# Expert weights split inside the expert loop, and a conditioning stage computed in transposed form

## What is computed

```
t   = lora(x) + emb                      # per batch, rank 16
q   = ffn0(t)                            # int8-style fake quantisation, 256 -> 704 -> 256, SiLU gate
x1  = x + q                              # 4096 rows of 256
h   = relu(x1 @ W1 + b1)                 # per batch, 64 wide
y   = x1 + h @ W2 + b2
z   = (y - mean(y)) * rsqrt(var(y) + 1e-5) * gamma + beta
logits = z @ Wr                          # 9 experts, the best two, softmax over them
moe = sum_k w_k * (silu(z @ Wg_k) * (z @ Wu_k)) @ Wd_k
out = x1 + moe
```

## Time and profile before

| | us |
|---|---|
| median of 3 runs (lowest, highest) | 803.58 (802.08, 804.01) |
| the profiled execution, its own time | 805.9 |
| its span | 804.1 |
| TensorE busy in the span | 672.1 (84%) |
| VectorE busy | 647.7 (81%) |
| ScalarE busy | 449.8 (56%) |
| GpSimd busy | 288.6 (36%) |

### The profile page before, as it was taken

One profiled execution on the slowest core, in us unless ns is written; L12 is line 12 of the kernel. 1 busy time (PEld: TensorE's weight loads), 2 busy tenths in 40 slices (PEclk: granted clock), 3 DMA queues, 4 the chain that ended last, 5 costly groups with the idle time before them and its releaser, 6 DMA issues.

```text
span 804.1 us, 16215 instructions
## 1 busy us (share of the span) xinstructions
PE 672.1 (84%) x4260; PEld 428.0 (53%) x4264; DVE 647.7 (81%) x1881; ACT 449.8 (56%) x801; POOL 288.6 (36%) x262
## 2 busy tenths in 40 slices
PE   6784876588877876219999999999999999999993
PEld 1212332354554545206767767776777767677762
DVE  6687888688999987837888888888888888888862
ACT  2675887578666645115555556555565655556540
POOL 1000455054688887720223222222322223232222
PEclk9665898578678665559999999999999999999996
DMA  6795112244566646863668677566666776766662
GB/s 211 267 363 192 62 37 75 66 151 144 173 192 186 184 141 189 260 223 65 104 103 114 105 99 121 101 114 106 112 108 96 114 104 111 114 104 107 109 89 38
DMA packets 163207, 107.63 MB, mean 134 GB/s; under 512 B 112940, under 2 KB 153012, under 8 KB 163124
## 3 DMA queue, kind: packets, MB, share of 16 engines
q1 hardware_dynamic: 149108, 88.10, 46.3%
q0 software_dynamic: 13440, 17.97, 12.8%
q10 hardware_dynamic: 576, 0.53, 0.2%
HBM read 50.31 MB, written 30.30 MB: 100 GB/s over the span
## 4 chain that ended last, share of the span: by engine, by line
PE 40%; issue 8%; DMA 6%; DVE 1%; POOLq 1%; ACT 1%; SPq 1%; POOL 0%; DVEq 0%; ACTq 0%
PE ps L1036 25%; PE ps L1078 13%; DMA out<-small 4%; PE ps L1020 2%; DMA rows<-small 1%; POOLq L1103 1%; POOL out L1096 0%; DVE small L1047 0%; SPq L972 0%; ACT small L1052 0%; DMA small<-rows 0%; ACT small L1060 0%; POOLq L73 0%; SPq L973 0%; DVE small L1066 0%
## 5 line engine op out<-in xcount | busy, mean ns | idle before, releaser
L1036 PE MATMUL ps<-big,small 128*128 x1728 | 273.2, 315 | 1.6 <-ACT small L1042 1.0
L1096 POOL DMA_INDIRECT out<-small x72 | 111.9, 1554 | 337.2 <-DVE small L1092 295.5
L1036 PEld LDWEIGHTS ps<-big,small 128*128 128x128 f16 x1728 | 164.0, 98 | 93.1 <-issue 2.6
L1078 PE MATMUL ps<-big,small 128*128 (+1 forms) x1224 | 156.4, 277 | 4.7 <-DVE small L1092 4.7
L1052 ACT ACTIVATE small<-small 128x704 f16<-128x704 f32 x72 | 56.9, 790 | 169.0 <-DVE small L1047 169.0
L1078 PEld LDWEIGHTS ps<-big,small 128*128 128x128 f16 (+1 forms) x1224 | 117.7, 99 | 34.3 <-issue 21.2
L1066 DVE SCALAR_TENSOR_TENSOR small<-small 128x64 f16<-128x64 f32 (+1 forms) x144 | 77.8, 582 | 18.8 <-ACT small L1060 18.8
L1047 DVE SCALAR_TENSOR_TENSOR small<-ps,small 128x704 f32<-128x704 f32 x72 | 68.5, 951 | 18.8 <-PE ps L1036 18.8
L858 POOL DMA_INDIRECT rows<-small x64 | 73.5, 1148 | 19.9 <-issue 16.7
L1060 ACT ACTIVATE small<-small 128x704 f16<-128x704 f32 x72 | 63.5, 882 | 16.2 <-DVE small L322 16.2
L609 PE MATMUL ps<-small 128*128 128x512 bf16 x188 | 50.2, 428 | 15.5 <-DVE small L585 9.0
(11 more groups left out here) (156 smaller groups left out, 1038.5 us busy)
## 6 DMA issues: line engine op xcount, KB each, us to landing
small<-rows SPq DMA_DIRECT2D x72, 130.0 KB, 2.1
big<-in_Wg SPq DMA_DIRECT2D x9, 704.0 KB, 4.2
big<-in_Wu SPq DMA_DIRECT2D x9, 704.0 KB, 4.2
big<-in_Wd SPq DMA_DIRECT2D x9, 640.0 KB, 8.2
halves<-big SPq DMA_DIRECT2D x6, 704.0 KB, 4.0
small<-in_xT SPq DMA_DIRECT2D x8, 512.0 KB, 4.0
small<-in_x SPq DMA_DIRECT2D x16, 256.0 KB, 4.1
out<-big SPq DMA_DIRECT2D x16, 256.0 KB, 4.2
```

The costliest lines, as they stand in the source:

```text
L1036: m = put("pe", ("gate", "up")[j], [tk["xsT", t], free, *wload, hl["hi", 26], hl["lo", 26]], lambda e, h=h, k=k, xp=xp, wp=wp, n=n: e.matm ...
L1078: tk["dn", t] = put("pe", "dn", [tk["hT", t], mk("yw", t - 1)], lambda e, n=n, w=w, hc_=hc_, wp=wp, c=c: e.matmul(ps[:, 7, 0:H], hTE[t % 3 ...
L1096: tk["add", t] = dma("pool", f"add{t % 2}", [tk["yw", t], *out_ready], lambda e: e.indirect_dma_start(out=out[:, :], out_offset=bass.Indir ...
```

## The change

- The nine early pieces are no longer split in the front, nor are any in the conditioning stage. `half_load` reads an expert's weights by its number from a table `permI`, sorted by how many rows the first six batches send to an expert. Six pieces are loaded after step 16; three are split before tile 0, the other 24 within the iterations 0 to 46 (`begin`), one about every two iterations: sum of squares in iteration `begin`, column sum (now bf16, one product), scale and high half in the next one, the low half in two parts in the two after that. The stores to HBM and the nine reloads of parts are gone.
- Tiles 0 to 4 belong to the fullest expert and start after step 19, before the last batch is routed; the tables are computed in iterations 0 to 3. Tile 5 waits for all scatters and paddings.
- The down product of the first network gives the transposed block; `st_x1T` adds x transposed. `st_px` is a real product with the identity, which carries nine logit columns and one column for the mean (`TG`), and the adapter product adds to the same PSUM banks (`W2S` with the same ten columns). So the transposes of the normalised rows, their evacuation and the logit products go. Their coefficients are made once by 16 small products (`through_adapter`) behind the gate and up stage, four elementwise products and `centre` in the front.
- The variance is a sum of squares on ScalarE (`st_squares`, one step after the adapter product); gamma is applied on VectorE with the evacuation, the scale and beta in one more operation each (`st_aff`); GpSimd has the power and the scatters left. The clip after quantisation is half on ScalarE (a second 128 x 1536 operation, from block 2 on) and half on VectorE.
- All rows share one power of two, worked out at the head of the conditioning stage from gamma and beta, so that the row scales of a tile (L999 to L1006) go. The row weights (L1084 to L1088) move to GpSimd (`side`, `weigh`).

The core of the diff:

```diff
-        hl, stored = {}, {}
+        hl = {}
+        AHEAD = 6
...
-            return bigf[:, o:o + PW[pieces[n][1]]]
+
+            k, j = divmod(n, 3)
+            o = 3 * EW + n * SLOT if n < AHEAD else 8 * EW + sum(PW[:j])
+            return raw8[:, 0:PW[j]] if k == E - 1 else bigf[:, o:o + PW[j]]
...
         def halves_out(n):
 
-            e_, j = pieces[n]
+            k, j = divmod(n, 3)
             w = PW[j] // 2
-            if n < EARLY:
-                o = (EARLY + n % 4) * SLOT
-                hi, lo = bigf[:, o:o + w], bigf[:, o + w:o + 2 * w]
...
+        def half_sum(n, waits=()):
+
+            m = put("act", "hsum", [hl["in", n], *waits], lambda e: e.activation(
+                halves_out(n)[0], slot_in(n), ACT.Square, accum_out=col(wsum, n)))
+            hl["sum", n] = put("act", "hsum", [m], lambda e: e.activation(col(wsb, n), col(wsum, n), ACT.Copy))
+
+        def top(n):
+            return ps[:, 7 if n < 3 else 5, 0:1]
+
+        def half_top(n):
+            hl["top", n] = put("pe", "htopp", [hl["sum", n], hl.get(("sc", n - 1)), tk["relu", S - 1] if n == 0 else tk["sq", S - 1] if n == 3 else None], lambda e: e.matmul(
+                top(n), onesb, col(wsb, n), start=True, stop=True))
...
+        def half_hi(n):
+            hl["hi", n] = put("act", "hhi", [hl["sc", n]], lambda e: e.activation(
                 halves_out(n)[0], slot_in(n), ACT.Copy, scale=col(wsc, n)))
...
+        def half_lo(n, part=(0, 1)):
+            w = PW[n % 3]
             hi, lo = halves_out(n)
-            hl["lo", n] = m = put("dve", "hlo", [hl["hi", n]], lambda e: e.scalar_tensor_tensor(
-                lo, slot_in(n), col(wsc, n), hi, ALU.mult, ALU.subtract))
-            if j == 2:
-                hl["lo", n] = m = put("dve", "hlo", [m], lambda e: e.tensor_copy(lo[64:128, 5 * H:6 * H], hi[64:128, 5 * H:6 * H]))
-            if n >= EARLY:
...
+        def unscale(n):
+
+            k, j = divmod(n, 3)
+            src = col(wun if j == 2 else wunx, n)
...
         def st_hq(s):
             v = hB[:, s // 2, :, 256 * (s % 2):256 * (s % 2) + 256]
-            m = put("dve", "hq", [mk("hy", s), mk("pd", s - 2), *l0], lambda e: e.tensor_scalar(
-                hq[:, s % 2], v, MAGIC + 127.0, MAGIC, ALU.min, ALU.subtract))
...
+            else:
+                tk["hq", s] = put("dve", "hq", [tk["hu", s]], lambda e: e.tensor_scalar(
+                    hq[:, s % 2], hq[:, s % 2], 255.0, -128.0, ALU.min, ALU.add))
...
+        def st_x1T(s):
+            for k in range(2):
+                tk["x1T", s] = put("dve", "x1T", [mk("pd", s), ksd, mk("xk", s), mk("hd", s - 2)], lambda e, k=k: e.scalar_tensor_tensor(
+                    x1T[:, s % 2, k, :], ps[:, s % 2, 256 * k:256 * k + 256], SD[:, k:k + 1],
+                    xk[:, s % 2, 256 * k:256 * k + 256], ALU.mult, ALU.add))
...
+        def st_px(s):
+            b = s // 2
+            for t in range(2):
+                for k in range(2):
+                    tk["px", s] = put("pe", "px", [tk["x1T", s], mk("sq", s - 2), kg, kti, tk["xun"]], lambda e, t=t, k=k: e.matmul(
+                        psY(s, t)[:, P * k:P * k + P + EC], x1T[:, s % 2, k, P * t:P * t + P],
+                        TG[:, b, 0:P + EC] if k else TG[:, b, EC:2 * EC + P],
+                        start=(k == 0), stop=True, skip_group_check=True))
+
...
         def st_x1(s):
-            v = x1[:, s % 3, :]
-            m = put("dve", "x1", [mk("pd", s), ksd, mk("y", s - 3), mk("xst", s - 3)], lambda e: e.tensor_tensor(
-                v.rearrange("p (t n) -> p t n", t=2), ps[:, s % 2, :].rearrange("p (t n) -> p t n", t=2),
-                SD.rearrange("p (a n) -> p a n", a=1).to_broadcast([P, 2, H]), ALU.mult))
...
+            tk["x1", s] = put("act", "x1", [mk("px", s), mk("xst", s - 3)], lambda e: e.activation(
+                x1[:, s % 3, :].rearrange("p (t a n) -> p t a n", t=2, a=2),
+                both.rearrange("p t (a n) -> p t a n", a=2)[:, :, :, 0:P], ACT.Copy))
 
...
-                    ps[:, 4, 256 * t:256 * t + 256], hT1[0:65, s % 2, P * t:P * t + P], W2S[0:65, b % 3, :],
-                    start=True, stop=True))
+                tk["ad", s] = put("pe", "ad", [tk["relu", s], tk["x1", s], kone, mk("par", b), tk["w2s", b]], lambda e, t=t: e.matmul(
+                    psY(s, t)[:, 0:H + EC], hT1[0:65, s % 2, P * t:P * t + P], W2S[0:65, b % 3, 0:H + EC],
+                    start=False, stop=True, skip_group_check=True))
 
...
+        def st_squares(s):
             r = s % 2
             for t in range(2):
-                tk["nrm", s] = put("act", "nrm", [mk("rstd", s)], lambda e, t=t: e.activation(
-                    yb[:, r, 256 * t:256 * t + 256], yb[:, r, 256 * t:256 * t + 256], ACT.Identity,
-                    bias=nb[:, r, t:t + 1], scale=rstd[:, r, t:t + 1]))
+                tk["sq", s] = put("act", "sq", [tk["g", s], mk("var", s - 2), mk("sq", s - 1)], lambda e, t=t: e.activation(
+                    halves(sqj[:, t, :]), psC(s, t), ACT.Square, bias=yl[:, r, t, E:EC], accum_out=ssq[:, r, t:t + 1]))
...
-            rb, odd = divmod(i - 6, 2)
+            rb, odd = divmod(i - 5, 2)
+            at(4, st_squares)
+            at(2, st_x1T)
+            at(1, st_hq)
+            at(4, st_var)
...
+            if 0 <= rb < NB and odd:
+                st_pos(rb)
+            at(2, st_px)
+            at(2, st_hd)
+            at(2, st_x1)
+            at(2, st_relu)
+            at(1, st_down)
+            at(2, st_ad)
+            if i % 2 == 1 and i < 2 * NB:
+                adapter_gate(i // 2)
+            at(0, st_hy)
+            at(3, st_ln)
+            at(4, st_logit)
             at(4, st_aff)
-            at(2, st_x1)
-            at(1, st_hq)
...
-            tk["xs", t] = dma("sp", f"xs{t % 9}", [tab, *rows_ready, mk("add", t - 9)], rows)
-
-        def x_bound(t):
...
+        def converted(t, j):
+
+            return [hl[w, 3 * k + j] for k in range(E) if -(-16 * k // 3) <= t for w in ("hi", "lo")]
...
+        def side(t):
+            x_, w_ = xs_(t), wt_(t)
+            put("pool", "wc", [tk["xs", t], mk("add", t - 9)], lambda e: e.tensor_copy(tok_(t), x_[:, 259:260].bitcast(I32)))
+            m = put("pool", "wc", [mk("yw", t - 9), tk["first"] if t < SOLO else tk["slotF"]], lambda e: e.tensor_scalar(
+                w_[:, 0:1], x_[:, 258:259], slotF[:, t:t + 1], 1.0, ALU.is_equal, ALU.subtract))
+            put("pool", "wc", [m], lambda e: e.tensor_scalar(w_[:, 1:2], w_[:, 0:1], x_[:, 257:258], None, ALU.mult))
+            tk["wc", t] = put("pool", "wc", [m], lambda e: e.tensor_scalar(w_[:, 2:3], w_[:, 0:1], 1.0, x_[:, 256:257], ALU.add, ALU.mult))
...
+        half_scale(2)
+        half_hi(2)
+        x_hi(0)
+        half_lo(1)
+        x_lo(0)
+        turn_rows(0)
+        evac_rows(0)
...
+        half_lo(2)
+        cond(20)
...
+        begin = {3: 0, 4: 2, 5: 4, 6: 5, 7: 7, 8: 8, 9: 10, 10: 12, 11: 13}
+        begin.update({n: 2 * n - 9 for n in range(12, 3 * E - 3)})
+        begin.update({3 * E - 3: 38, 3 * E - 2: 41, 3 * E - 1: 44})
...
             on(1, times)
-            on(-2, x_scale)
+            piece(3, lambda n: half_lo(n, (1,)) if n in split else None)
+            piece(2, lambda n: half_lo(n, (0,) if n in split else (0, 1)))
...
+            piece(1, half_top)
             on(-1, turn_rows)
+            on(-2, x_lo)
             on(-1, evac_rows)
-            on(-2, x_lo)
...
+            on(-2, side)
+            piece(1, half_scale)
+            piece(1, half_hi)
+            piece(0, lambda n: half_sum(n, [hl["lo", AHEAD - 1]] if n >= 9 else []))
...
+            if t < len(chunks):
+                chunks[t]()
+            for n in range(3, 3 * E):
+                if max(begin[n] + 1, len(chunks) - 1) == t:
+                    unscale(n)
```

820 lines of the change are left out of this document (432 added, 388 removed).

## The result

Four runs of the changed kernel took 757.12 to 762.39 us, median 759.28; four of the kernel before on the same chip 801.51 to 804.01, median 802.83. The ratio is 0.946, with a 95% interval of 0.942 to 0.951: 43.6 us less. The forecast was 757, the profiled span is 760.7 us where 757.6 was summed up; the profiled execution is the longest of the four.

The account below looks back on a forecast made before the run. TensorE was taken to bound the expert loop, with VectorE busy 62.0 of 65 us in a stretch ahead of it. Profiled span 804.1 - 11 + 1.5 - 45.5 (second scale to first down product) + 8.5 = 757.6, median 757 us; range 733 to 787.

Parts of the forecast that it names:

- Front, -11: Up to the first scale: nine pieces leave ScalarE and VectorE, 11 us less; -4 or -19 depending on the low clock.
- Gate and up, +1.5: First to second scale: 16 small products (32 passes, 5.4 us) where TensorE idles 4.8 us; 0 to +3.5, taken as +1.5.
- Second scale to step 4: 24: Start of conditioning: load of gamma and beta, small operations, then three steps mostly at TensorE's low clock; 24 us (20 to 28).
- Steps, 8.2 us: Conditioning steps 4 to 16: ScalarE's own loop, 8.2 us each (bounds 7.4 and 9.4) against 10.5; 106.6 us in all.
- Behind the steps, 31: After step 16: three pieces loaded and split beside steps 17 to 19, 31 us (26 to 38); then 25 to first down product.
- Loop, +8.5: Expert loop: piece work fits beside TensorE's 5.87 us per tile; column sums 3.5, tables 2, DMA 3 (0 to 20).
- signs by which the sum was to be called wrong: Passes 10 us apart, TensorE in the loop waiting for ScalarE or a transposing DMA, or iteration 3 waiting for rows.
- rival 1: TensorE's clock stays low in the dense conditioning steps: 9.4 us each, front only -4; 780 us, chance 0.12.
- rival 2: TensorE's clock rises and stays up: conditioning steps of 7.4 us, front -19; 738 us, chance 0.08.
- Rival 3: Expert loop becomes VectorE's or the DMA's: order costs 0.5 us in each of 42 iterations, +21; 778 us, chance 0.13.
- Rival 4: Slower than before: no loop piece work hidden, 2.7 us of VectorE per piece, +65; 818 us, chance 0.05.
- Rival 5: The five early tiles overlap nothing: tile 5 waits 15 us longer for scatters and paddings; 772 us, chance 0.04.

Follow-up runs that it names:

- yardstick: The changed kernel run once more with no edit: ratio 0.9393 to the kernel before, six runs of 755.56 to 768.52 us, median 758.53.

## Why the prediction was right

The total was right, within 3.1 us of the profiled span and 2.3 of the median. Its parts were right only in part, and some of their errors cancelled.

- **Front, -11.** Measured -4.3, the value given for a low clock in all batches; the yardstick's profile has -18.7, close to the -19 given for one that ends after the first. The -11 was worked out as if the low clock would end where it did in the one profile of the kernel before, at 50.6 us. But where it ends differs between executions: among the ten profiles with this front and no added products at 35 or 36 us (four), 43, 50 and 57 us, or not at all (three), with the first scale between 55.2 and 69.8. Their mean is 62.1 us, near the 63 of the forecast. So the term was a fair mean and could not be right for a single execution; that the profiled one drew the slow end is chance. The last maximum came 1.3 us behind the end of the last expansion, where it had come 5.6 behind, as counted.
- **Gate and up, +1.5.** Measured +0.1 (71.4 for 71.3), near its lower bound; in the yardstick +1.0. The 32 passes for the adapter coefficients took 2.0 us, where 5.4 were given, and ended 2.6 us before the scale's product.
- **Second scale to step 4: 24, measured 29.9.** Above the range of 20 to 28. TensorE was at 0.67 there, as forecast, but the stretch was priced as three steps and a dozen small operations and not followed along its chain. In the rows the small operations and gamma's and beta's load hold VectorE until 6.5 us behind the scale (5.6 given). The first block then goes through alone: VectorE's passes, the down product (3.08 us), `x1T`, the identity products (2.21), and ScalarE waits 11.24 us for them. The last of the three steps takes 8.2 us.
- **Steps, 8.2 us.** Measured 85.93 / 11 = 7.8, and 8.3 in the yardstick. The closed loop on ScalarE was the right mechanism: to give it the wait to fill brought 9.3 us, to take its second pass away 16.6. Its sums are met at both levels, 7.4 at the high clock by a step of 7.0 and 9.2 at the low one by a step of 8.9. What was off is the share of the levels: the clock was 0.90 where 0.74 was taken over from the kernel before.
- **Behind the steps, 31 to the first gate product.** The first load of a piece went out at 267.5, 96.7 us behind step 4 (106.6 given). Of the 9.9 us, 5 are the shorter steps; the rest is that the load went out in the midst of step 16, while the sum counted that step to its end. From there it was 28.3 us (31 given), then 27.0 (25 given). The place of the first gate product, near 297, was 295.8, and of the first down product, near 323, 322.8. That is luck: the errors of 5.9, -9.9, -2.7 and 2.0 us cancelled in part against each other and against the front's 6.7.
- **Loop, +8.5.** Measured +11.2, of which 8.8 lie behind the down product of tile 2 and 2.4 in the two tiles ahead of it (the tables had been given 2). The step of the prediction that failed is the one by which the wide piece operations fit beside TensorE's 5.87 us since the busy times add up to less: they were priced at nothing and cost 9.0 us. The column sums (3.5 given) and the DMA (3 given) cost nothing that shows: a column sum takes 0.03 us of TensorE, and behind tile 2 TensorE waits for no transposing DMA but 0.9 us ahead of the last down product, though the DMA share was 0.92 from 420 to 520 us. The size was right for the wrong reason. VectorE was busy 84.2 of these 100 us, a little below the 85 to 90 given. Two of the signs by which the sum was to be called wrong were there: TensorE waited 5.2 us for ScalarE in the loop, and 4.2 for tile 0's transposing DMA.
- **Rivals.** Neither rival 1 nor rival 2 came as a whole. The front went by rival 1 in the first profile and by rival 2 in the yardstick's; the steps stayed between 7.4 and 9.4 in both, and the two spans differ by 2.6 us. The rule cited for rival 2, from the Trainium skill's "TensorE: Matmul & The Clock Gate" (HAM oscillation), held for the gate product behind 3.3 us of waiting. It did not hold for the front, where TensorE had no gap from 32 to 64 us and stayed at the low clock; there the measurement decides. Rival 3 had the right mechanism for the loop, that order costs what the busy sums hide, at more than twice its price: 0.5 us in each of 42 iterations against 9.0 / 42 = 0.2. Rival 4's 1.9 us per piece stand against 0.4. Rival 5's 15 us did not come: with the early tiles taken away the kernel is 3 us slower by the medians (-1 to 8), so they bring little, but what they wait for was already in the 31 + 25 that the sum had for these stretches.

## What to carry to other kernels

Where several engines are each busy some three quarters of a stretch, follow one operation through every engine's queue until the same operation of the next step. The step is as long as that loop. Taking a pass out of it or moving it into a wait shortened the stage here (9 to 17 us), and a reorder closed a longer loop (52 us). To price work that is put beside a full engine, keep the operations and make them narrow: to take a single wait away only moves it (4.5 us gone, 3.4 come). And profile the same program twice before a stage is compared: here 14 us of a front belonged to the execution, not to the edit.

## What the runs showed of the hardware

Two of the small operations that were moved to GpSimd (L1157 and L1158, one column each) take 0.29 and 0.26 us alone, and at times much longer; L1157 took 1.70 once. (The two ahead of them, L1154 and L1155, start while GpSimd's own indirect DMA is being issued, and take 0.88 and 1.20 us on average.) At 550 us both engines stand in the rows of the changed kernel, GpSimd first, then VectorE:

```profile
550.06 1.70 POOL L1157 TENSOR_SCALAR small<-small 128x1 f32<-128x1 f32 x1
```
```profile
549.91 1.68 DVE L396 SCALAR_TENSOR_TENSOR big<-small,big 128x1408 f16<-128x1408 f32 x1
```

GpSimd's operation starts under VectorE's low half, which reads two tiles of SBUF, and ends 0.17 us behind it. It is so in the next longest cases too: 0.97 us at 350.80 under a low half of 0.95, 0.71 us at 491.22 under the hidden low halves (L1136), both ended 0.17 us behind VectorE. In the 33 of 67 cases in which no VectorE operation with two inputs in SBUF overlaps it, L1157 takes 0.29 us each time. The Trainium skill has a rule for this ("SBUF — State Buffer", Who interferes with whom): a VectorE instruction with two SBUF inputs contends with a GpSimd instruction that reads SBUF, and the ports that they share are locked, not divided. The trace agrees (0.29 us alone, 1.70 beside 1.68). No experiment here took it apart, and no wait of TensorE was put down to it.
